# Adding a bias row to resident activations by one accumulating DMA instead of by two engines, with four moves in the order of instructions

## The reference

```
x   = x + attn_block(layernorm(x))
x   = x + moe_block(layernorm(x))

attn_block(x):  low = x
  twice:        l, h = dwconv(low, h_filter)[::2], dwconv(low, g_filter)[::2]; keep h; low = l
  low = linear_attention(low, 16 heads)
  twice:        low = dwconv(repeat(low, 2), h_synth) + dwconv(repeat(h, 2), g_synth)
  return layer_norm(x + low) * norm_gamma + norm_beta

moe_block(x):   16 experts; every expert takes the 256 tokens of highest sigmoid score (top_k per expert),
                gathers them, silu(gate) * up -> down, scales by the score, scatter-adds;
                plus a shared expert, silu(x W1) * (x W2) W3
```

## Time and profile before

| what | us |
| --- | --- |
| median of three timed executions (214.26 to 214.61) | 214.35 |
| the profiled execution, whole | 215.54 |
| its span | 213.6 |
| PE busy in it | 182.9 (86%) |
| DVE busy | 129.6 (61%) |
| POOL busy | 121.6 (57%) |
| ACT busy | 89.5 (42%) |

### The profile page before, as it was taken

How to read it: one execution, slowest core, us unless ns; L and a number is a source line. 1 busy time by engine, 2 the same in 40 slices (tenths; PEclk the granted TensorE clock), 3 DMA queues, 4 the chain that set the end, 5 groups by cost and what they waited for, 6 DMA issues and landing times.

```text
span 213.6 us, 3635 instructions
## 1 busy us (share of the span) xinstructions
PE 182.9 (86%) x1210; PEld 158.7 (74%) x1210; DVE 129.6 (61%) x431; ACT 89.5 (42%) x238; POOL 121.6 (57%) x175
## 2 busy tenths in 40 slices
PE   7789889999979899789899999999998899989000
PEld 7758769999836676559799999999897799978000
DVE  4879999999678888798444444444424444444000
ACT  0676603267586765110034444444434344434100
POOL 7610006546044467504776788878788777775550
PEclk9999999999999999996999999999999999999655
DMA  5699999500300550101422333323333233332221
GB/s 149 209 418 425 414 413 420 228 0 3 110 3 0 150 208 2 49 3 52 115 64 49 38 44 43 48 43 51 38 41 44 37 37 42 38 38 28 25 25 12
DMA packets 11618, 22.21 MB, mean 104 GB/s; under 512 B 1488, under 2 KB 8784, under 8 KB 11472
## 3 DMA queue, kind: packets, MB, share of 16 engines
q1 hardware_dynamic: 5968, 17.52, 21.6%
q0 software_dynamic: 5632, 4.46, 15.3%
HBM read 17.65 MB, written 4.33 MB: 103 GB/s over the span
## 4 chain that ended last, share of the span: by engine, by line
PE 44%; DVE 17%; DMA 14%; POOL 9%; issue 8%; ACT 3%; POOLq 1%; SPq 1%; DVEq 0%
DMA out_dram<-area,rows 11%; PE bank L1341 7%; PE bank L1342 7%; PE bank L1326 6%; PE bank L1080 6%; POOL out_dram L486 6%; PE bank L1035 4%; DVE junk L888 4%; DMA x_tok<-in_x_dram 2%; POOL sh_hid L460 2%; PE bank L1233 2%; PE bank L1097 2%; PE bank L1183 2%; DMA hT<-h_rows,rows 1%; DVE area L739 1%
## 5 line engine op out<-in xcount | busy, mean ns | idle before, releaser
L486 POOL DMA_INDIRECT out_dram<-area,rows x32 | 50.6, 1582 | 17.5 <-DMA out_dram<-area,rows 9.4
L1020 DVE SCALAR_TENSOR_TENSOR area<-bank,consts,sgate 128x256 f32<-128x256 f32 x64 | 30.9, 483 | 40.5 <-ACT sgate L670 40.5
L670 ACT ACTIVATE sgate<-bank,consts 128x256 f32<-128x256 f32 x64 | 30.2, 472 | 59.5 <-PE bank L1342 59.5
L1326 PEld LDWEIGHTS bank<-wT,area 128*128 128x128 f32 x256 | 38.4, 191 | 3.6 <-DVE area L1020 0.4
L1341 PE MATMUL bank<-area,wT 128*128 128x256 f32 x128 | 38.5, 383 | 1.6 <-issue 1.4
L1326 PE MATMUL bank<-wT,area 128*128 128x128 f32 x256 | 38.8, 275 | 0.2 <-DVE area L1020 0.2
L474 POOL DMA_INDIRECT hT<-h_rows,rows x32 | 32.0, 1000 | 11.4 <-issue 8.8
L1342 PE MATMUL bank<-area,wT 128*128 128x256 f32 x128 | 38.1, 379 | 0.0
L1342 PEld LDWEIGHTS bank<-area,wT 128*128 128x128 f32 x128 | 24.3, 190 | 3.3
L1035 PE MATMUL bank<-ident 128*128 128x128 f32 x164 | 23.9, 306 | 1.6 <-POOL ident L381 1.6
L1035 PEld LDWEIGHTS bank<-ident 128*128 128x128 f32 x164 | 22.4, 219 | 2.2 <-POOL ident L381 1.6
(11 more groups left out here) (186 smaller groups left out, 252.3 us busy)
## 6 DMA issues: line engine op xcount, KB each, us to landing
wT<-in_weights_dram SPq DMA_DIRECT2D x16, 768.0 KB, 16.5
h_rows<-hrow SPq DMA_DIRECT2D x2, 576.0 KB, 3.3
x_tok<-in_x_dram SPq DMA_DIRECT2D x4, 256.0 KB, 3.9
x_tok<-in_down_b_dram SPq DMA_DIRECT2D x1, 1024.0 KB, 7.2
out_dram<-x SPq DMA_DIRECT2D x4, 256.0 KB, 2.7
hT<-h_rows,rows POOLq DMA_INDIRECT x32, 2.6
out_dram<-area,rows POOLq DMA_INDIRECT x32, 3.3
sh_wT<-in_shared_dram SPq DMA_DIRECT2D x1, 384.0 KB, 2.9
```

What stands on the lines that cost most here:

```text
L486: pool.indirect_dma_start(out=out_rows, in_=eo[:, e % 2, c, :], in_offset=None, out_offset=bass.IndirectOffsetOnAxis(ap=rows[:, g, c, k:k ...
L670: act.activation(sgate_e[:, q % SGB, :], up_bank(q)[:, CAP:2 * CAP], ACT.Silu, bias=biasT[:, 1, j, e:e + 1]).then_inc(s_sil, 1)
L1020: dve.scalar_tensor_tensor(hidden[:, e % 2, j, :], up_bank(q)[:, 0:CAP], biasT[:, 0, j, e:e + 1], sgate_e[:, q % SGB, :], ALU.add, ALU.mul ...
L1326: last = pe.matmul(bank[3 + e % 2][:, c * P:(c + 1) * P], hidden[:, e % 2, j, c * P:(c + 1) * P], wT[:, e, 2, j, :], start=(j == 0 and c = ...
```

## The change

Six edits. beta is added to all 16 tiles of x_tok by one DMA that POOL issues, with an adding write; it starts once both readers of x_tok are done, and DVE waits for it once, ahead of group 0. POOL's four adds and DVE's three `add_beta` are gone. On ACT, the second sigmoid and `keep_hT(0)` move behind round 0's `count_third`. On DVE, the first multiplication for r1p moves behind the masked sums, and `level1_even(2)` behind attention's result. WARM_C goes from 10 to 4.

```diff
@@ POOL
             norm_scale(norm_no("x", 1))
+            pool.wait_ge(s_xnv, NB)
             pool.wait_ge(s_xna, NB)
-            pool.wait_ge(s_r1v, 1)
-            for i in range(8, 12):
-                last = pool.tensor_tensor(x_tok[:, i, :], x_tok[:, i, :], beta_bc, ALU.add)
-            last.then_inc(s_beta, 1)
+            pool.dma_start(x_tok[:, :, :], beta_bc.unsqueeze(1).to_broadcast([P, NT, C]),
+                           accum_op=ALU.add).then_inc(s_beta, 16)
             sum_scale(0)
@@ ACT
                            ACT.Sigmoid).then_inc(s_score, 1)
-            act.activation(hrow[:, :, C:ROW].rearrange("p (k r) e -> p k r e", r=2),
-                           logits[:, :].rearrange("p (r e k) -> p k r e", r=2, e=E), ACT.Sigmoid).then_inc(s_hrow, 1)
-            keep_hT(0)
...
                 count_third(r)
+                if r == 0:
+                    act.activation(hrow[:, :, C:ROW].rearrange("p (k r) e -> p k r e", r=2),
+                                   logits[:, :].rearrange("p (r e k) -> p k r e", r=2, e=E), ACT.Sigmoid).then_inc(s_hrow, 1)
+                    keep_hT(0)
@@ DVE
-            link(dve.tensor_scalar(r1_even, h2p[:, :, 0:N2], tap_sum(1, 0), None, ALU.mult))
             dve.wait_ge(s_masks, 1)
...
                               same8[:, :].unsqueeze(1).to_broadcast([P, NB, P]), ALU.mult).then_inc(s_kvm, 1)
+            link(dve.tensor_scalar(r1_even, h2p[:, :, 0:N2], tap_sum(1, 0), None, ALU.mult))
             link(level1_even(1, r1_even))
-            link(level1_even(2, r1_even))
...
                                   ALU.mult).then_inc(s_attn, 1)
+            link(level1_even(2, r1_even))
...
-            dve.wait_ge(s_xna, NB)
-            add_beta(0)
-            add_beta(1)
+            dve.wait_ge(s_beta, 16)
...
-                if g == 2:
-                    dve.wait_ge(s_beta, 1)
-                if g == LAST:
-                    add_beta(LAST)
                 block_out(g)
@@ PE
-            WARM_I, WARM_E, WARM_S, WARM_L, WARM_C = 5, 3, 6, 3, 10
+            WARM_I, WARM_E, WARM_S, WARM_L, WARM_C = 5, 3, 6, 3, 4
```

More of the change, by code:

```diff
@@ L814, in _ @@
             finish_even(1)
-            def add_beta(g):
-                dve.tensor_tensor(x_tok[:, group(g), :], x_tok[:, group(g), :],
-                                  beta_bc.unsqueeze(1).to_broadcast([P, 4, C]), ALU.add)
-            dve.wait_ge(s_xna, NB)
-            add_beta(0)
-            add_beta(1)
+            dve.wait_ge(s_beta, 16)
             def x1_t(i):
```

## The result

The changed kernel takes 226.44 us (median of four timed executions, 226.01 to 226.69) against 214.48 (214.26 to 215.81) for the kernel before beside it: 1.051 times as long, 95% interval 1.047 to 1.056. Slower by some 12 us; the forecast was 223.1 with 228.8 as its upper end. The profiled execution took 226.69 us against 215.54, so the two traces have 11.15 us between them to explain.

What follows compares the result with a forecast made beforehand. Prediction: PE bounds 33 to 54 us, then a search chain through PE, DVE and ACT. DVE's wait +9.8 and search -1.1 give +8.7: 214.35 + 8.7 = 223.1 us; range 213.0 to 228.8.

Steps and rivals of the forecast that it cites:

- The landing: Beta's DMA ahead of DVE's group 0: ends at 49.0 us, so group 0 starts 10.4 us later than 38.56.
- One packet for each row: Beta's adding DMA: rows not merged, 2048 packets of 512 B, 128 on each of 16 engines.
- Not ahead of the weights: Beta's rows beside the expert weights: served by turns, one packet of each queue, or behind the weights; both end at 49.0.
- All work shared out: DMA engines: beta outlasts the weights and ends when all work is done, 42.0 + 7.0 = 49.0 us.
- When the rows begin: Start of beta's rows: once POOL has issued the DMA, 14.3 + 1.6 us in the served-at-once bound.
- The rival of a hidden transfer: Beta's DMA lands between 23 and 38 us, unseen by DVE; only the search's gain remains, 213.25 us; chance 0.24.
- The rival of a held POOL: POOL kept in the issue until the last rows are taken, `sum_scale(0)` after the wait: 224.5 us; no separate chance.
- From group 0 to the logits: Stretch behind the wait: DVE reaches the last group 9.8 us late; PE, 8.6 late, doesn't add.
- The clock: PE after idling before `turn_x1(0)`: 3 to 4 us at 1.2 GHz, synthesis up to 1.7 us longer; cost 0 to 0.8, taken 0.
- The search: Round 0's decision: 1.1 us earlier from WARM_C and ACT's order, handed on to the end; -0.5 without ACT's order.
- that rival: Clock falls in the search: some 2 us over two or three rounds; chance 0.08 together with a middle landing.
- rows of 92 ns: Slow bound for beta's rows on each DMA engine: 11.8 us for 128 rows, the wait ending at 53.8.

Runs made afterwards that it cites:

- experiment 3: Changed kernel, but SP issues four of the sixteen weight loads and holds the other twelve until beta has landed: 215.62 us, 1.000 of before.
- experiment 4: Changed kernel, but four copies of beta lie side by side, so the DMA adds 512 rows of 2 KB: 215.86 us, 1.002 of before.
- experiment 6: Changed kernel, but beta added by four DMAs, each with its own semaphore, DVE waiting for each group apart: 217.0 us, 1.007 of before.
- experiment 5: Changed kernel plus 36 matmuls on the identity on PE ahead of `turn_x1(0)`, to hold the clock up: 228.0 us, 1.057 of before.
- experiment 2: Kernel before with only the accumulating DMA and its wait, the other edits left out: 226.87 us, 1.054 of before.
- experiment 1: Changed kernel with beta added by DVE and POOL as before, the other edits kept: 214.29 us, 0.995 of before.
- experiment 7: Kernel before with WARM_C 4 instead of 10 and nothing else: 213.58 us, a single time.
- experiment 8: Kernel before with only ACT's sigmoid and copy of hT moved behind round 0's third count: 214.62 us, a single time.

## Why the prediction was right, point by point

**The landing** was put at 49.0 and came at 49.01. The steps behind it hold, but for when the rows begin. *One packet for each row:* q0 has 2064 packets in after, 2048 rows and 16 semaphores. *Not ahead of the weights:* q1 and q0 from 22 to 33 us (packets, MB, share of 16 engines):

```profile
q1 hardware_dynamic: 667, 3.66, 85.2%
q0 software_dynamic: 666, 0.34, 24.2%
```

667 packets of weights and 666 of beta: strictly by turns, one each, 61 in a microsecond of either kind. By bytes the split is 11 to 1. The Trainium skill, "DMA: Bandwidth & Descriptors", section "Queues, rings and completion order", states this turn of one packet per queue, and the trace agrees. *All work shared out:* the weights end at 47.1 instead of 42.0 (the prediction said near 49), the last rows at 48.7, about the 42.0 + 7.0 of the sum; by the 58 ns a row of experiment 3 the 7.0 would be 7.4. *When the rows begin* was not seen: the prediction let them begin when POOL had issued the DMA, some 16 us, and the first row moved at 20.5, 3.2 us after POOL's row ends. In experiment 3, without weights beside it, the first row moved at 17.7, 0.6 us after. What holds the first rows back beside the weights was not tried. The landing doesn't hang on it, because the work still to do decides the end: at 61 rows in a microsecond, 2048 rows begun at 20.5 would have lasted until 54, but the weights ran out first and the rows then had the engines to themselves (372 rows between 46 and 48 us, against some 122 in two microseconds before). Experiments 3, 4 and 6 each change one factor (who takes turns, how many turns, how many rows a wait stands for) and move the wait by what the turns say.

The rival of a hidden transfer rested in part on bytes. The Trainium skill's fit for DMAs from POOL's queue ("DMA: Bandwidth & Descriptors", section "Anatomy of one DMA — SWDGE (gpsimd) path") gives some 4.4 us from issue to landing for a megabyte, an estimate; measured are 34.2 beside the weights and 11.6 without, so here the measurement decides against it. The rival of a held POOL is out too: its row is 2.5 us, and `sum_scale(0)` wasn't late (its power begins at 36.93, before at 37.12).

**From group 0 to the logits** the sum followed DVE, 9.8 late, and set PE aside as 8.6 late. DVE's own part is right: at the full clock it reaches the last group 9.99 us after group 0 (experiment 5), 49.01 + 9.99 = 59.00 in the times of after, 9.86 later than before. PE's 8.80 is right too.

**The clock** is the step that was mis-sized: "cost 0 to 0.8, I take 0". Two sizes were off. PE lost 2.23 us: 1.75 in the 40 rows, as said, and 0.48 in `turn_x1(0)` ahead of them, since the lower level lasted 10.2 us and not 3 to 4. And PE had 9.8 - 8.8 = 1.0 us to spare instead of 1.2. So PE, and not DVE, set the logits: 8.80 + 2.23 = 11.03, 1.2 over the 9.8 of the sum. Experiment 2, with a shorter stretch at the lower level, gives the same sum with other numbers (8.92 + 1.45).

**The search** was put at -1.1, and -0.5 without ACT's order: measured -1.13 and -0.51, and PE's wait for hT 0.62 against 0.5. The granted clock was 1.00 from 58 to 96 us, through the search, so that rival is out.

**What was missing** is the last +1.26. The chain of after shows it, start us and us, among its scatter-adds:

```profile
172.94 3.19 DMA out_dram<-area,rows
...
178.28 3.29 DMA out_dram<-area,rows
...
183.72 4.60 DMA out_dram<-area,rows
...
190.47 3.28 DMA out_dram<-area,rows
```

One landing takes 1.3 us longer, and the scatter-add at 188.59 waits for it. Into that landing falls one packet of instruction fetch on q8, 0.97 us long on one engine, at 186.32. The same was found in each of the ten profiles: of all scatter-adds, eleven had their last row more than 2 us after POOL's issue ended (some 1.4 is usual), and in all eleven a q8 packet lies in the landing. The reverse doesn't hold: some fifteen other landings have a q8 packet among their rows too and were not late by that measure (1.4 to 1.9 us). It costs time only where the next scatter-add waits for just that one: once in after and in experiments 3 and 4 (1.3 to 1.7 us), twice in experiment 5, not in before and not in 1, 6, 7 and 8; in experiment 2 the late one costs nothing, and another with a q8 packet costs 0.5 us. A late landing as such is in all ten profiles, but time was lost in five of the six kernels with the adding DMA and in none of the four without it. Experiments 3 and 4, in which DVE doesn't wait for the DMA, took 1.3 and 1.6 us more in the median than experiment 1, which has no such DMA. So whether the 1.26 are chance or a second cost of the DMA stays open. That the fetch causes the delay was not tried either; it is a coincidence, without exception in one direction only.

Together: 8.80 + 2.23 - 1.13 + 1.26 = 11.16 us, against 11.15 between the two profiled executions. Of the 2.5 us that the sum of 8.7 lacks, 1.2 are the clock and 1.3 the scatter-add. The median missed its forecast by 3.3 us: these 2.5, and 0.8 from the two profiled executions, which lie at different heights over their medians. That 226.44 is inside the range is in part luck: the upper end was set by rows of 92 ns, which did not come (58 measured), and by 0.8 for the clock; what filled that room was a clock term of 1.2 and a late landing that the prediction did not have.

## What to carry to other kernels

Count packets, not bytes: beside a full queue the DMA of small rows got one packet for each packet of the other here (666 beside 667), so it ends after rows divided by the other queue's packet rate, or when all work is done, whichever is first; here it was the second. Give it long rows (landing after 19.7 us instead of 34.2), or several semaphores so that the first user waits for its own part only (217.0 us instead of 226.4); neither was faster than the adds on the engines. And before work is taken off an engine, look whether it stands in idle time: here the adds that were saved had cost nothing, and the wait that came for them stood on the path.

## What the runs showed of the hardware that was not expected

- In after, rows of 512 B between weight packets of mostly 6 KB cost the weights a fifth of their rate: 333 GB/s (3.66 MB in 11 us) against 418, while beta got 31 GB/s. Both together moved 365 GB/s.
- The first row of the DMA moved 3.2 us after POOL's issue ended in after (17.27 to 20.51) and 3.3 us after it with rows of 2 KB (16.10 to 19.44), both beside the weights, and 0.6 us after it alone (17.17 to 17.74, experiment 3).
- Issuing one DMA from POOL took 2.50 us for 2048 rows, 1.54 us for 512 rows, and 5.48 us for four DMAs of 512 rows: it grows with rows only slowly, far from the 25 us of the upper bound.
- An adding DMA of 2 KB rows was not split into smaller packets: 528 packets for 512 rows.
- After PE's idle time the lower clock lasted 4.6 us into PE's work in after, and in experiment 5 it fell for 3.4 us in a stretch in which PE had no idle time of its own; in the 3.8 us ahead of it (56.90 to 60.69) PE had been idle for 0.40 us.
